# A transformer block on Trainium2: the transposition of a unit's row maxima by one matmul instead of four, and their copy moved from ScalarE to VectorE

## The reference

```python
xn = _layernorm(x, axis=-1)
x = x + _L0_attn_ref(xn, ...) + _L0_ffn_ref(xn, ...)

# attention, per head (D = 64)
att = jnp.einsum('bqhd,bkhd->bhqk', q, k) * scale / temperature
bias = slopes[:, None, None] * rel[None, :, :]
bias = jnp.where(causal[None, :, :], bias, -jnp.inf)
w = jax.nn.softmax(att + bias[None, :, :, :], axis=-1)
y = jnp.einsum('bhqk,bkhd->bqhd', w, v).reshape(Bc, Tc, Cc)
return y @ W_proj + b_proj

# feed-forward, HIDDEN = 3072, integer weights scaled by 1/127
h = jax.nn.silu(gate) * up
return jnp.einsum('bsh,dh->bsd', h, wd)
```

## Time and profile before

| what | value |
|---|---|
| median of 3 runs | 1149.74 us (1149.16 to 1150.83) |
| the profiled execution | 1151.06 us |
| its span, first to last instruction of the slowest core (core 1) | 1149.5 us |
| spans of the eight cores | 1144.0 to 1149.5 us |
| TensorE's granted clock, mean of the span | 0.997 to 1.000 |

### The profile page before, as it was taken

One profiled execution on the slowest core, in us unless ns is written; L12 is line 12 of the kernel. 1 busy time (PEld: TensorE's weight loads), 2 busy tenths in 40 slices (PEclk: granted clock), 3 DMA queues, 4 the chain that ended last, 5 costly groups with the idle time before them and its releaser, 6 DMA issues.

```text
span 1149.5 us, 24412 instructions; the slowest of 8 cores (1144.0 to 1149.5 us)
## 1 busy us (share of the span) xinstructions
PE 1101.4 (96%) x7702; PEld 562.9 (49%) x7702; DVE 585.8 (51%) x1190; ACT 516.1 (45%) x933; POOL 266.6 (23%) x289
## 2 busy tenths in 40 slices
PE   3899899999999999999999999999999999999998
PEld 1344455555555555555555555555555344444443
DVE  5441766666666676676666666666773100000110
ACT  1443456655655665565565566556666200000000
POOL 6210121222221222132222112112223432222220
PEclk9999999999999999999999999999999999999999
DMA  8439033433413432153321313113521652525222
GB/s 181 134 89 178 20 61 70 75 75 66 88 35 66 80 79 65 39 89 70 65 57 29 66 43 62 34 31 69 170 61 33 220 188 74 183 74 183 74 74 74
DMA packets 57055, 98.37 MB, mean 86 GB/s; under 512 B 23284, under 2 KB 43893, under 8 KB 55846
## 3 DMA queue, kind: packets, MB, share of 16 engines
q0 software_dynamic: 7872, 35.66, 16.5%
q1 hardware_dynamic: 46178, 52.65, 15.7%
q10 hardware_dynamic: 2884, 8.50, 1.9%
HBM read 90.49 MB, written 27.26 MB: 102 GB/s over the span
## 4 chain that ended last, share of the span: by engine, by line
PE 88%; DVE 5%; issue 3%; DMA 2%; ACT 1%; POOL 1%; DVEq 0%; ACTq 0%; POOLq 0%; SPq 0%
PE ps_gu L724 25%; PE ps_dn L885 14%; PE ps_s L815 10%; PE ps_t L796 10%; PE ps_m L704 9%; PE ps_y L831 5%; PE ps_dn L880 5%; PE ps_t L764 5%; DVE cm L553 2%; DMA xstage<-xin 2%; PE ps_m L844 1%; PE ps_s L818 1%; PE ps_t L800 1%; DVE st L501 1%; DVE hst L489 1%
## 5 line engine op out<-in xcount | busy, mean ns | idle before, releaser
L553 DVE TENSOR_REDUCE cm<-ps_s 128x1 f32<-128x512 f32 (+3 forms) x640 | 379.9, 608 | 195.0 <-PE ps_s L815 112.0
L660 ACT ACTIVATE pt<-ps_t 128x512 bf16<-128x512 f32 (+1 forms) x576 | 327.2, 575 | 241.6 <-PE ps_t L796 151.3
L724 PE MATMUL ps_gu<-xnT,wubuf 128*128 128x512 bf16 x768 | 262.0, 378 | 2.3 <-DVE hst L489 2.3
L724 PE MATMUL ps_gu<-xnT,wgbuf 128*128 128x512 bf16 x768 | 261.3, 378 | 1.2 <-ACT kst L605 1.2
L815 PE MATMUL ps_s<-kx,qx 67*128 67x512 bf16 (+3 forms) x640 | 213.5, 347 | 9.7 <-DVE cm L553 8.2
L796 PE MATMUL ps_t<-qx,kx 98*128 98x512 bf16 (+3 forms) x640 | 216.4, 348 | 2.0 <-ACT pt L660 1.8
L431 POOL TENSOR_SCALAR th_s<-th_s 128x512 f32<-128x512 f32 x96 | 59.1, 616 | 621.4 <-ACT th_s L613 621.4
L885 PE MATMUL ps_dn<-wdres,hb 128*128 128x512 bf16 x768 | 168.5, 379 | 0.0
L831 PEld LDWEIGHTS ps_y<-Vt,pt 128*128 128x128 bf16 x2176 | 125.3, 97 | 81.9
L831 PE MATMUL ps_y<-Vt,pt 128*128 128x65 bf16 x2176 | 138.8, 193 | 0.0
L594 DVE SCALAR_TENSOR_TENSOR outsb<-ps_dn,xres 128x512 f32<-128x512 f32 x32 | 20.7, 686 | 205.1 <-PE ps_dn L885 205.1
(11 more groups left out here) (74 smaller groups left out, 753.8 us busy)
## 6 DMA issues: line engine op xcount, KB each, us to landing
h_sc<-hst SPq DMA_DIRECT2D x96, 128.0 KB, 1.8
hb<-h_sc SPq DMA_DIRECT2D x4, 3072.0 KB, 14.0
xstage<-xin SPq DMA_DIRECT2D x16, 512.0 KB, 6.1
xres<-xin POOLq DMA_DIRECT2D x16, 512.0 KB, 4.8
out<-outsb ACTq DMA_DIRECT2D x15, 512.0 KB, 2.7
wgbuf<-wg_r POOLq DMA_DIRECT2D x12, 512.0 KB, 6.3
wubuf<-wu_r POOLq DMA_DIRECT2D x12, 512.0 KB, 8.9
wd_sc<-wd_r POOLq DMA_DIRECT2D x12, 512.0 KB, 8.1
```

Source lines behind the costliest of these rows:

```text
L553: e.tensor_reduce(cm[:, c0:c0 + 1], ps_s[:, s % 2 * 512:s % 2 * 512 + w], AX.X, AluOpType.max, negate=True).then_inc(sem["v_mx"], 1)
L660: e.activation(pt[t % NPT][:, 0:w], ps_t[:, t % 2 * 512:t % 2 * 512 + w], AF.Exp).then_inc(sem["a_e"], 1)
L724: mm = e.matmul(ps_gu[:, r // 8 * 512:r // 8 * 512 + 512], w[:, w0:w0 + 128], xnT[:, dc * T + tb * 512:dc * T + tb * 512 + 512], start=(dc ...
```

## The change

One matmul now transposes all the maxima of a unit. The tile `nm` has KT = 104 columns instead of 4 x 98; columns 96 to 103 hold the eight columns (i, c), tile i and part c (value or remainder). Transposed against the identity they give partitions 96 to 103 of `ps_m`, 128 columns wide, partition 96 + 2i + c belonging to tile i. VectorE then spreads them: it reads these 8 x 128 values four times over (a broadcast over the tiles i') and multiplies with a constant 0/1 tile, `tile_s`, that is 1 where i' = i. The result, 8 partitions by 512 columns of bfloat16, goes to rows 96 to 103 of `qx`; each query's column has its two parts in two of the eight rows and zeros in the other six. `kx` holds ones in all eight rows, and L796 contracts 104 rows. ACT's copy and its semaphore `a_m` are gone; `v_m` of VectorE takes their place, in the waits of PE for `ps_m` and for the first L796 of a unit. The constant `tiles` comes by a fifth transfer on ACT's queue.

```diff
-KT = 98
+KT = 104
...
-        nm = [sb(st, f"nm{i}", [128, 4 * KT], BF16) for i in range(2)]
+        tile_s = sb(st, "tile_s", [128, 512], BF16)
+        nm = [sb(st, f"nm{i}", [128, KT], BF16) for i in range(2)]
...
-                m_users.append(("a_m", M[1] + 1))
+                m_users.append(("v_m", M[1] + 1))
...
-                    e.memset(kx[q][j][96:98, :], 1.0).then_inc(sem["g_set"], 1)
+                    e.memset(kx[q][j][96:KT, :], 1.0).then_inc(sem["g_set"], 1)
...
-                        n3 = nm[par].rearrange("p (i c) -> p i c", c=KT)
+                        n3 = nm[par][:, 96:KT].rearrange("p (i c) -> p i c", c=2)
...
-                        e.tensor_copy(n3[:, :, 96:97], src).then_inc(sem["v_mc"], 1)
+                        e.tensor_copy(n3[:, :, 0:1], src).then_inc(sem["v_mc"], 1)
                         e.wait_ge(sem["v_mc"], c + 1)
-                        e.tensor_tensor(n3[:, :, 97:98], src, n3[:, :, 96:97], AluOpType.subtract)
+                        e.tensor_tensor(n3[:, :, 1:2], src, n3[:, :, 0:1], AluOpType.subtract)
...
+                if M is not None and M[0] == "m":
+                    n = M[1]
+                    h, b = n // 4, n % 4
+                    e.wait_ge(sem["p_m"], n + 1)
+                    e.tensor_tensor(
+                        qx[h // 2 % 2][h % 2][96:KT, b * 512:(b + 1) * 512].rearrange("p (i q) -> p i q", i=4),
+                        ps_m[96:KT, 0:128].unsqueeze(1).broadcast_to([8, 4, 128]),
+                        tile_s[96:KT, :].rearrange("p (i q) -> p i q", i=4), AluOpType.mult).then_inc(
+                            sem["v_m"], 1)
                 for f in units_ended(k, 15):
                     gate_times_up(f)
...
-                             (bqk_s[:, :], battn_qk[:, :]), (mask_s[:, :], masks[:, :])):
+                             (bqk_s[:, :], battn_qk[:, :]), (mask_s[:, :], masks[:, :]),
+                             (tile_s[96:KT, :], tiles[:, :])):
...
-                if M[0] == "m":
-                    n = M[1]
-                    h, b = n // 4, n % 4
-                    e.wait_ge(sem["p_m"], n + 1)
-                    e.activation(qx[h // 2 % 2][h % 2][96:98, b * 512:(b + 1) * 512], ps_m[96:98, :],
-                                 AF.Copy).then_inc(sem["a_m"], 1)
...
-                        e.wait_ge(sem["a_m"], n + 1)
+                        e.wait_ge(sem["v_m"], n + 1)
...
-                    for i in range(4):
-                        mm = e.matmul(ps_m[0:KT, i * 128:(i + 1) * 128], nm[n % 2][:, i * KT:(i + 1) * KT],
-                                      ident_s[:, :], start=(i == 0), stop=(i == 3))
-                    mm.then_inc(sem["p_m"], 1)
+                    e.matmul(ps_m[0:KT, 0:128], nm[n % 2][:, :], ident_s[:, :], start=True,
+                             stop=True).then_inc(sem["p_m"], 1)
...
+    tiles = np.repeat(np.repeat(np.eye(4, dtype=np.float32), 2, axis=0), 128, axis=1)
```

More of the change, by code:

```diff
@@ L42 @@
     "g_set", "g_th", "g_s", "g_xr",
[L46 to L49 removed]
+    "v_t", "v_cbq", "v_ln", "v_xn", "v_q", "v_mx", "v_mc", "v_m", "v_rc", "v_y", "v_h", "v_out",
+    "a_c", "a_sd", "a_xe", "a_v", "a_k", "a_e", "a_th", "a_g", "a_b",
     "p_c", "p_xT", "p_v", "p_qk", "p_s", "p_m", "p_t", "p_av", "p_g", "p_u", "p_b", "p_d", "p_dl",
@@ L167, in build_program @@
     masks = din("masks", [128, 256], BF16)
+    tiles = din("tiles", [8, 512], BF16)
     slopes = din("slopes", [H, 3, T], BF16)
@@ L665, in _ @@
                     continue
[L666 to L672 removed]
+                if M[0] == "qk" and M[2] and M[1] % 2:
                     evac_k(M[1] // 8 + 1, M[1] % 8 // 2)
@@ L929, in _consts @@
         "masks": masks.astype(BF),
+        "tiles": tiles.astype(BF),
         "slopes": np.ascontiguousarray(np.stack(parts, axis=1)),
```

9 lines of the change are left out of this document (3 added, 6 removed).

## The result

| | before | changed |
|---|---|---|
| ratio of the times, undisturbed runs | 1 | 0.9956, 95% interval 0.994 to 0.9972 |
| the profiled execution | 1151.06 us | 1145.15 us |
| its span (slowest core) | 1149.5 us | 1143.6 us |
| attention stage, median of the 8 cores | 770.8 us | 765.6 us |

The change makes the kernel 0.44% faster; 0.9956 of the five runs' median before, 1150.83 us, is 1145.8 us. The forecast was 1142.5, the range 1137.5 to 1148. (The ratio leaves out runs in which one die ran at a lower clock than the other, three of the changed kernel's five and none of the five before, so that it rests on two runs after the change, 1145.15 and 1144.54 us.)

A forecast was written before the change was run, and what follows sets the result against it. PE, busy 96%, was taken as the bound, with VectorE second at some places. PE's saving, VectorE's loss and the rest, -11.0 + 3.8 + 0 = -7.2 us, gave 1142.5 us from a median of 1149.74; range 1137.5 to 1148.

The forecast's parts named there:

- PE's saving: Attention stage: one transposing matmul per unit instead of four, at a pitch of 0.06 us, saves 11.0 us.
- The lower bound: Remaining transpose holds PE for its whole 124 ns load: 0.116 us saved per unit, 7.4 us in all.
- the upper ones: PE's saving if every removed weight load counted, 23.8 us; by the skill's 81 ns per matmul, 15.6 us.
- K of 104: Score matmuls L796 contract 104 rows instead of 98: no cost.
- The pass's length and its place in the queue: New VectorE pass takes 0.69 us per unit, 44 us in all, taken as not overlapping its neighbours.
- The 16 tight units: Pass behind the following unit's last reduction, cast and subtraction delays the next reduction: 0.24 us each, 3.8 us lost.
- the one worked out: One tight unit near 400 us: slack 0.78 us, reduction ends 402.04, PE wants it by 401.80, loss 0.24 us.
- "Price 0" for the 48 others: In 48 units the pass stands in 0.54 us of VectorE idle time; the double score buffer covers it, cost 0.
- ACT's relief: 64 removed ACT copies, 37.8 us of ACT time, let exponentials start sooner: gain between 0 and 5.8 us, taken as 0.
- The scores' wait for the pass: A unit's scores (L796) wait for the pass instead of ACT's copy; the pass is in time, price 0.
- The signs that I had named: PE's waits for L553 and L815's issue, 48.8 us, grow about 4; over 11 means slower (chance 0.08).
- The opening: Fifth constant transfer on ACT's queue (3.25 + 0.58 us) precedes its semaphore's first reader at 13.95 us: price 0.

The follow-up runs named there:

- e3: The changed kernel with a second VectorE pass of the same size right behind the first, into a scratch tile; stage 784.2 us, ratio 1.0115.
- e7: The changed kernel with cast and subtraction of the 16 b = 0 units one step later, behind the next reductions; stage 759.5 us, ratio 0.9901.
- e10: The changed kernel with an ACT copy of 2 x 512 elements per unit kept, into scratch; stage 768.9 us, ratio 0.9982.
- e5: The changed kernel with the VectorE pass of only the b = 3 units one step later; stage 772.2 us, ratio 1.0009.
- e2: The changed kernel with the one transpose issued four times, so the pass without PE's saving; stage 771.8 us, no ratio given.
- e9: The kernel before the change with cast and subtraction of the 16 b = 0 units one step later; stage 770.4 us, ratio 0.9992.
- e11: The changed kernel with the cast written as a tensor_tensor max of the source with itself; stage 765.4 us, ratio 0.9956.
- e8: The changed kernel with the cast chain of all 64 units one step later, behind the next reductions; stage 757.6 us, ratio 0.9889.

## Why the prediction was right, and where not

Its mechanism held: PE's stream sets the time, and VectorE's pass gives part of the saving back where it delays a reduction. The sizes of the single terms did not all hold, and part of the nearness is luck, as the sum shows.

**PE's saving: right.** 11.0 us were forecast from a pitch of 0.06; the mean over 64 units is 0.059 for one of four, 0.072 for the single one, together 10.5 us. The lower bound (the one that stays holds PE for its load of 124 ns) and the upper ones were both off. The Trainium skill's 81 ns per matmul ("TensorE: Matmul & The Clock Gate", "Back-to-back issue gap") does not hold here: 59 ns.

**K of 104: right.** 380 ns at 512 columns, as in the earlier trace rows.

**The pass's length and its place in the queue: right.** 0.697 us forecast as 0.69, and started only when its forerunner had ended, its follower after it; e3 shows the same operation overlapping its follower when the partitions agree. The Trainium skill's rule ("VectorE: DVE Perf Modes", "Two Vector instructions with no wait between them") agrees with every one of these starts.

**The 16 tight units: right in place and kind, too small.** 3.8 us were forecast (0.24 each at 16 places); 0.38 each at 15 were measured, 5.7 us. At the one worked out, the pass and the reduction stood as drawn, and it lost 0.34: 0.09 more because the signal takes 0.15 us and not the 0.06 that I had assumed without a row, 0.03 because the reduction ended 2.87 us after the transpose instead of 2.84, less 0.02 because PE had saved 0.16 and not 0.18. The rest is the spread between places, which one place can't tell: seven lost 0.33 or 0.34, but the units 11 and 15 lost 0.88 and 0.71. e7 takes this loss away whole.

**"Price 0" for the 48 others: wrong by some 3 us.** With ACT's relief taken out (e10) the intervals from b = 1 have lost 0.7 us and those from b = 2 2.2; those from b = 0 are whole in sum, since 0.65 us lost behind unit 0 meets 0.8 gained behind unit 20, where the long cast is gone. The first three units alone lose 1.6 us. Of the 2.2 us behind b = 2, 1.1 is PE's saving itself, lost at the seven units whose next score tile was already held before the change. I worked out one ordinary step and let it stand for 48.

**ACT's relief, "I take 0": wrong by 3.3 us.** I gave bounds of 0 and 5.8 and took 0 since no ACT line showed in the chain of the stage. The chain gives one way through the stage, and its printed line breaks off at shares of 0.4%; 0.4% of 754 us would be 3 us.

**The scores' wait for the pass: the reckoning was wrong, the price 0 came out by luck.** I reckoned its end to be "in time" without naming the deadline or the signal. PE's scores were in fact held by it at 14 of the 15 places, and it cost nothing only because the reduction behind the pass held the next tile longer; that removing this wait alone would give nothing is read from the starts, no run does it. e5 shows that a later pass costs at once.

**The sum.** It was -11.0 + 3.8 + 0 = -7.2 us. The runs give -10.5 (PE), -3.3 (ACT) and, as the rest to the stage's -5.2, +8.6. These 8.6 us are the pass and what of PE's saving never arrives; by e2 4.2 of them are there only with the saving. That is 4.8 more than forecast, and ACT's relief, forecast as 0, covers 3.3 of it: two errors of opposite sign left the stage's forecast 2 us too low. So it was partly luck that the time, 1145.8 us, fell into the range. As a ratio the forecast was 1142.5 / 1149.74 = 0.9937, just below the measured interval.

**The signs that I had named.** The sum of the waits before the score tiles was to grow by 4 us, and by more than 11 the change would be slower. It grew by 15.1 (48.8 to 63.9) and the change was faster. That sum is mostly idle time of the weight loads, and it counts time in which PE is still at work: the weight loads' share alone is 52.3 us, while PE's own idle time in the stage is 754.00 - 732.97 = 21.0 us. In e2 the sum grew by 8 us, and the stage by 1.

**The opening.** I had the transfer of the tiles as free because its first reader came at 13.95 us. That was read on core 1, the one core of eight without a wait there. On the other seven VectorE waited 0.7 to 2.5 us for the mask before, and on all eight it waits 0.2 to 2.6 us for the tiles now. The start of the stage scatters over the same 5 us in both kernels, so no run settles whether the transfer costs anything.

## What to carry to other kernels

Work that moves to an engine with idle time has to be placed by its two deadlines, that of who waits for it and that of what stands behind it in the queue. Here two tiny instructions that nobody waited for yet, the cast and the subtraction, stood ahead of both; putting it one step later gave nothing by itself (e9, 0.4 us) and more than the change itself when both were made (e7, 6.1 us on top of 5.2). And a stage whose length repeats to 0.1 or 0.2 us on eight cores, as in most of these kernels, is a better gauge than the run's time, in which 5 us of scatter from the opening lie. Last, an instruction that starts at the least distance from another's end, here 0.15 us, was in all likelihood waiting for it, even where the list of waits doesn't name it.

## What the hardware showed beside that

In every trace ten or eleven of the 64 casts last two to seven times as long as the others (0.33 to 1.18 us; nearly all others 0.16 to 0.18), and end with a POOL instruction that had started before them, within 0.05 us. POOL and VectorE of the changed kernel:

```profile
803.35 1.16 POOL L439 TENSOR_TENSOR gs_s<-th_s,gh_s 128x512 bf16<-128x512 f32 x1 [0.27 <-POOL th_s L433]
```

```profile
803.55 0.97 DVE L575 CAST nm<-nmf 128x4 bf16<-128x4 f32 x1 [0.17 <-DVE nmf L566]
804.63 0.17 DVE L577 TENSOR_TENSOR nm<-nmf,nm 128x4 bf16<-128x4 f32 x1
```

The cast is done at 804.52 instead of 803.72; POOL's instruction ends at 804.51. All four operands involved lie in SBUF; the reductions of scores, the pass and the gate product, which read PSUM, never show it (the pass: 696 to 699 ns over all 64). Nor does the minimum L566, though it reads and writes SBUF: 160 to 171 ns over 48, seven of them in the midst of a POOL instruction. I had thought it a matter of the copy form; e11 shows that a tensor_tensor does the same, and in e8, where it meets POOL, the subtraction took up to 0.93 us in place of 0.17. How much of the stage that costs was not tried; together the long casts take 4.9 us more of VectorE in the changed kernel.
